# GRU state update: a product and a sum replaced by one running product-sum over interleaved pairs

## The reference, cut to what matters

```python
def cell(h, x):
    gi = x @ W_ih + b_ih
    gh = h @ W_hh + b_hh
    i_r, i_z, i_n = jnp.split(gi, 3, axis=-1)
    h_r, h_z, h_n = jnp.split(gh, 3, axis=-1)
    r = jax.nn.sigmoid(i_r + h_r)
    z = jax.nn.sigmoid(i_z + h_z)
    n = jnp.tanh(i_n + r * h_n)
    h_new = (1.0 - z) * n + z * h
    return (h_new, h_new)
...
x = x + _L3_cond_ref(cond_2048, x, ...)
```

## Time and profile before

| | |
|---|---|
| median of 3 runs | 2069.48 us (2069.31 to 2070.36) |
| the profiled execution, its own time | 2070.81 us |
| its span, first to last instruction | 2069.1 us |
| first and last `h_hi` (L1663) of the 127 in the GRU's steps | 1700.4 us, 2056.0 us |
| mean time of a step between them | 2.82 us |

### The profile page before, as it was taken

The page is one execution under the profiler, slowest core; times in us unless marked ns, Lnnn a source line. Parts: engine busy times, 40 slices in busy tenths (PEclk is TensorE's granted clock), DMA queues, the critical chain, the costliest instruction groups (busy, mean ns, idle before and its releaser), DMA issues. The chain is left out here.

```text
span 2069.1 us, 48431 instructions
## 1 busy us (share of the span) xinstructions
PE 1437.8 (69%) x16570; PEld 1116.0 (54%) x16570; DVE 1418.7 (69%) x6953; ACT 742.6 (36%) x2889; POOL 591.5 (29%) x1597
## 2 busy tenths in 40 slices
PE   6898844444444444445599999999957866677665
PEld 4476533333333333332488888888825754555554
DVE  4457699989989998997556555555546345555554
ACT  4568522222222222223334333433344443333322
POOL 1045355545545554553311111111124000000010
PEclk9979955555555555556799999999988975555555
DMA  3000000000000000002100000000020000000000
GB/s 108 0 1 2 1 2 2 2 3 2 2 3 2 2 2 3 2 2 87 46 1 31 16 18 15 16 1 1 1 81 31 1 0 2 2 2 13 4 11 23
DMA packets 15097, 28.20 MB, mean 14 GB/s; under 512 B 1692, under 2 KB 9464, under 8 KB 14584
## 3 DMA queue, kind: packets, MB, share of 16 engines
q1 hardware_dynamic: 14672, 24.93, 3.5%
q10 hardware_dynamic: 168, 0.04, 0.0%
HBM read 20.77 MB, written 4.19 MB: 12 GB/s over the span
## 5 line engine op out<-in xcount | busy, mean ns | idle before, releaser
L817 PE MATMUL bank<-s_tanh_hi,coup_hi 128*128 128x16 f16 x2048 | 141.6, 180 | 344.6 <-ACT s_tanh_hi L807 329.5
L817 PEld LDWEIGHTS bank<-s_tanh_hi,coup_hi 128*128 128x128 f16 x2048 | 95.0, 108 | 392.0 <-ACT s_tanh_hi L807 376.7
L807 ACT ACTIVATE s_tanh_hi<-s_s 128x32 f16<-128x32 f32 x384 | 88.0, 229 | 394.9 <-DVE s_s L679 394.9
L1245 POOL TENSOR_TENSOR prob<-prob,inv 128x512 f32<-128x512 f32 x64 | 66.5, 1040 | 426.4 <-DVE inv L1211 426.4
L1523 PE MATMUL bank<-h_hi,w_h_hi 128*128 128x16 f16 x1536 | 95.2, 176 | 111.6 <-DVE h_hi L1663 111.6
L1131 ACT ACTIVATE prob<-bank,neg_max 128x128 f32<-128x128 f32 x256 | 90.5, 366 | 215.5 <-DVE neg_max L1180 215.5
L1687 POOL TENSOR_TENSOR x<-x,h 128x32 f32<-128x32 f32 x128 | 34.4, 269 | 447.9 <-DVE h L1666 447.9
L817 PE MATMUL bank<-s_tanh_lo,coup_hi 128*128 128x16 f16 x2048 | 141.3, 180 | 22.3 <-DVE s_tanh_lo L673 9.7
L1523 PEld LDWEIGHTS bank<-h_hi,w_h_hi 128*128 128x128 f16 x1536 | 70.7, 105 | 158.0 <-DVE h_hi L1663 158.0
L817 PE MATMUL bank<-s_tanh_hi,coup_lo 128*128 128x16 f16 x2048 | 130.2, 174 | 0.0
L817 PEld LDWEIGHTS bank<-s_tanh_lo,coup_hi 128*128 128x128 f16 x2048 | 94.6, 107 | 61.9 <-DVE s_tanh_lo L673 33.8
(11 more groups left out here) (286 smaller groups left out, 4713.6 us busy)
## 6 DMA issues: line engine op xcount, KB each, us to landing
w_stage<-in_L_cond_qkv_w_dram SPq DMA_DIRECT2D x12, 512.0 KB, 5.2
x_tok<-in_x_dram SPq DMA_DIRECT2D x4, 512.0 KB, 5.8
ow_stage<-in_L_cond_out_w_dram SPq DMA_DIRECT2D x4, 512.0 KB, 5.4
x_in<-x SPq DMA_DIRECT2D x1, 2048.0 KB, 11.4
x_in_sb<-x_in SPq DMA_DIRECT2D x1, 2048.0 KB, 12.0
out_dram<-o_sb SPq DMA_DIRECT2D x64, 32.0 KB, 1.6
ada_w<-in_L_cond_ada_w_dram SPq DMA_DIRECT2D x1, 1536.0 KB, 12.2
v_bias<-in_L_cond_qkv_b_dram SPq DMA_DIRECT2D x4, 256.0 KB, 5.6
```

What stands on the lines that cost most here:

```text
L807: A.activation(th_hi[:, :], s, ACT.Tanh).then_inc(hi_ready, 1)
L817: ins = nc.tensor.matmul(coupled[:, B * m:B * m + B], w[:, o:o + P], th[:, B * c:B * c + B], start=(first and c == 0 and m == 0), stop=(la ...
L1245: G.tensor_tensor(prob[:, grp % 2, :, :], prob[:, grp % 2, :, :], inv[:, grp % 2, :].unsqueeze(2).broadcast_to([P, HG, T]), MUL).then_inc( ...
```

## The change: what it does

`cand` and `zh` become the even and the odd places of one f32 tile `cand_zh` of 128 x 64, and `keep` the odd places of a tile `zero_keep` whose even places are zero for good. The running product-sum takes state = keep_i * state + cz_i along the 64 places: at an even place the state becomes 0 * state + cand, at the odd place behind it keep * cand + zh, which is h. Its output is a tile of pairs too, whose odd places are h. It is done twice, once with an f16 output (`h_hi`) and once with an f32 output (`h32`). The instruction for `new` and its semaphore go. Readers of `h_hi` (PE, DVE) and of `h32` (DVE, POOL) now read every second element; ACT writes `cand`, and DVE `keep` and `zh`, at every second element. Before the steps there is one memset more.

```diff
-    h32 = [sb(f"h32_{i}", [P, W]) for i in range(2)]
-    h_hi, h_lo = sb("h_hi", [P, W], F16), sb("h_lo", [P, W], F16)
+    cz, kz = sb("cand_zh", [P, W, 2]), sb("zero_keep", [P, W, 2])
+    h32p = [sb(f"h32_{i}", [P, W, 2]) for i in range(2)]
+    h32 = [t[:, :, 1] for t in h32p]
+    h_hip, h_lo = sb("h_hi", [P, W, 2], F16), sb("h_lo", [P, W], F16)
+    h_hi = h_hip[:, :, 1]
+    cand, zh, keep = cz[:, :, 0], cz[:, :, 1], kz[:, :, 1]
+    pairs = lambda t: t[:, :, :].rearrange("p w k -> p (w k)")
...
+            V.memset(kz[:, :, :], 0.0).then_inc(keep_ready, 1)
+            dve.wait_ge(keep_ready, 1)
...
-                V.tensor_scalar(keep[:, :], z[:, :], -1.0, 1.0, MUL, ADD).then_inc(keep_ready, 1)
+                V.tensor_scalar(keep, z[:, :], -1.0, 1.0, MUL, ADD).then_inc(keep_ready, 1)
                 dve.wait_ge(h32_ready, s + 1)
-                V.tensor_tensor(zh[:, :], z[:, :], h32[s % 2][:, :], MUL).then_inc(zh_ready, 1)
-                dve.wait_ge(keep_ready, s + 1)
+                V.tensor_tensor(zh, z[:, :], h32[s % 2], MUL).then_inc(zh_ready, 1)
+                dve.wait_ge(keep_ready, s + 2)
                 dve.wait_ge(cand_ready, s + 1)
-                V.tensor_tensor(new[:, :], cand[:, :], keep[:, :], MUL).then_inc(new_ready, 1)
                 dve.wait_ge(zh_ready, s + 1)
-                dve.wait_ge(new_ready, s + 1)
                 dve.wait_ge(z_full, s + 1)
                 if s + 1 < T:
-                    V.tensor_tensor(h_hi[:, :], new[:, :], zh[:, :], ADD).then_inc(hhi_ready, 1)
+                    V.tensor_tensor_scan(pairs(h_hip), pairs(kz), pairs(cz), 0.0, MUL, ADD).then_inc(hhi_ready, 1)
                 if s >= 1:
                     dve.wait_ge(added, s)
-                V.tensor_tensor(h32[(s + 1) % 2][:, :], new[:, :], zh[:, :], ADD).then_inc(h32_ready, 1)
+                V.tensor_tensor_scan(pairs(h32p[(s + 1) % 2]), pairs(kz), pairs(cz), 0.0, MUL, ADD).then_inc(h32_ready, 1)
...
-                A.activation(cand[:, :], pre[:, :], ACT.Tanh).then_inc(cand_ready, 1)
+                A.activation(cand, pre[:, :], ACT.Tanh).then_inc(cand_ready, 1)
...
-                G.tensor_tensor(x4[:, lap % 2, :, :, j:j + 1], x3[:, :, :, s:s + 1], h32[(s + 1) % 2][:, :].rearrange("p (c b o) -> p c b o", c=C, o=1),
+                G.tensor_tensor(x4[:, lap % 2, :, :, j:j + 1], x3[:, :, :, s:s + 1], h32p[(s + 1) % 2][:, :, 1:2].rearrange("p (c b) o -> p c b o", c=C),
```

More of the change, by code:

```diff
@@ L1433, in gru @@
     gi_n = sb("gi_n", [P, T, C, B])
-    h32 = [sb(f"h32_{i}", [P, W]) for i in range(2)]
-    h_hi, h_lo = sb("h_hi", [P, W], F16), sb("h_lo", [P, W], F16)
+    cz, kz = sb("cand_zh", [P, W, 2]), sb("zero_keep", [P, W, 2])
[5 more added lines that the diff above has]
+    pairs = lambda t: t[:, :, :].rearrange("p w k -> p (w k)")
     r, z = sb("r3", [P, W]), sb("z3", [P, W])
-    rhn, pre, cand, keep, zh, new = (sb(n, [P, W]) for n in ("rhn", "pre", "cand", "keep", "zh", "new"))
+    rhn, pre = sb("rhn", [P, W]), sb("pre", [P, W])
     x4 = sb("x4", [P, 2, C, B, TB])
@@ L1445, in gru @@
     r_ready, z_ready, rhn_ready, pre_ready = sem("r_ready"), sem("z_ready"), sem("rhn_ready"), sem("pre_ready")
-    keep_ready, zh_ready, cand_ready, new_ready = sem("keep_ready"), sem("zh_ready"), sem("cand_ready"), sem("new_ready")
+    keep_ready, zh_ready, cand_ready = sem("keep_ready"), sem("zh_ready"), sem("cand_ready")
     added, o_last = sem("added"), sem("o_last3")
@@ L1628, in gates_low @@
                                        ADD, SUB).then_inc(gil_out, 1)
-            V.tensor_copy(h_hi[:, :], cond).then_inc(hhi_ready, 1)
-            V.tensor_copy(h32[0][:, :], cond).then_inc(h32_ready, 1)
+            V.tensor_copy(h_hi, cond).then_inc(hhi_ready, 1)
+            V.tensor_copy(h32[0], cond).then_inc(h32_ready, 1)
+            V.memset(kz[:, :, :], 0.0).then_inc(keep_ready, 1)
+            dve.wait_ge(keep_ready, 1)
             dve.wait_ge(hhi_ready, 1)
             dve.wait_ge(h32_ready, 1)
-            V.tensor_tensor(h_lo[:, :], h32[0][:, :], h_hi[:, :], SUB).then_inc(hlo_ready, 1)
+            V.tensor_tensor(h_lo[:, :], h32[0], h_hi, SUB).then_inc(hlo_ready, 1)
             for n in range(LAPS):
@@ L1669, in _ @@
                     dve.wait_ge(h32_ready, s + 2)
-                    V.tensor_tensor(h_lo[:, :], h32[(s + 1) % 2][:, :], h_hi[:, :], SUB).then_inc(hlo_ready, 1)
+                    V.tensor_tensor(h_lo[:, :], h32[(s + 1) % 2], h_hi, SUB).then_inc(hlo_ready, 1)
                 if s in unit_at and jobs[s][0] == "gi" and jobs[s][2] < 2 * C:
```

## The result

| | before | after |
|---|---|---|
| median | 2069.31 us (11 runs) | 2075.75 us (11 runs) |
| span of the profiled execution | 2069.1 us | 2073.9 us |
| ratio | | 1.0032, 95% interval 1.0022 to 1.0041 |

What follows compares the result with a forecast made beforehand. The GRU loop's DVE state-update chain, with PE waiting last for `h_lo`, was taken to bound 109 updates; 88 x 0.034 + 21 x 0.089 - 88 x 0.01 = 4.0 us off 2069.5 gave 2065.5 us, range 2054 to 2079.

Steps and rivals of the forecast that it cites:

- A wait comes forward: First running sum must wait for `zh`, which `new` did not: 0.055 us lost on each of 88 updates.
- the first sum holds the engine: Rival: second running sum can't start until the first ends; 5.2 us lost, 2074.7; 0.30 together with a larger fixed part.
- the 88 updates: State updates on the path (109) without the 21 where z was early; forecast to gain 0.034 us each at `h`.
- `new` goes: On DVE, the first running sum could start where `new` stood: 0.28 us gained on each of 109 updates.
- Half pace and overlap: Running sums at 2.02 ns a place, 96 ns more each; the second starts 0.205 us after the first, which still runs.
- The high bound: Running sum at the pace of `gi_lo`, taken as the trace's slowest element, 5 ns: 287 ns more each.
- the far rival: Running sums at 5 ns an element: 42 us slower, 2107; chance 0.05.
- Every second element: Operands stepping by two: only `zh` on the path pays, 0.01 us x 88; POOL's addition nothing.
- Unit steps: 18 GRU steps held by `gi_lo` or ACT's `gi_n`, not by the state update; forecast unchanged.
- POOL's start ahead of `h_lo`'s: POOL's addition starts 0.03 us before `h_lo`, which stays near 280 ns; rival of POOL second: 2055.7, chance 0.08.
- the gain of 0.034: Forecast gain in us at `h`, and with it at `h_lo`, on each of 88 updates, before `zh`'s 0.01.
- the updates with an early z: 21 updates where `new` waited for `cand` and `zh` was done early: no 0.055 us paid, 0.089 us gained each.

Runs made afterwards that it cites:

- waits-alone kernel: Kernel before, with the changed kernel's four waits (keep, cand, zh, z_full) ahead of `new` and only `new`'s wait ahead of `h_hi`: 2076.75 us, ratio 1.0041.
- order-alone: Changed kernel with the same four waits ahead of the first running sum, rewritten so zh's comes first and rides inline: 2065.57 us, ratio 0.9987.
- both pairs: Running sums against plain form, each with fewer waits (0.9960, 0.9972), then also with one semaphore for `h_hi` and `h` (0.9873, 0.9883).
- the best kernel: Changed kernel with two waits ahead of the running sum and one semaphore for `h_hi` and `h`: 2042.38 us, ratio 0.9873.

## Why the prediction was wrong

Its step that failed is "A wait comes forward": "with 0.10 us from end to start it allows 1854.165, 0.055 us after where `new` stood". The place was right and the size was not. I read the 0.10 us off pairs with two or three waits, as if it belonged to DVE, when it belonged to the place of the wait that is released last. Where that wait is inline it is 0.03 to 0.04 us: so `h_hi` behind `new` in the waits-alone kernel, and so, already in the trace of the kernel before, `pre` behind `rhn`:

```profile
1853.32 0.19 DVE L1647 SCALAR_TENSOR_TENSOR rhn<-bank,r 128x32 f32<-128x32 f32 x1 [0.67 <-ACT r L1596]
1853.55 0.19 DVE L1651 TENSOR_TENSOR pre<-rhn,gi_n 128x32 f32<-128x32 f32 x1
```

Where it is a wait instruction with no other behind it, it is 0.09 to 0.10 us; in the changed kernel one more stands behind it, and it is 0.20. So the first running sum began 0.155 us after where `new` stood, not 0.055. The prediction's rival of that sign, "the first sum holds the engine", gives a time close to the measured one, 2074.7, and is refuted: the sums overlap.

Point by point, on the 88 updates:

- *`new` goes*: right, 0.28 us gained.
- *The wait*: 0.155 lost, forecast 0.055. The order-alone and waits-alone kernels show it from both sides.
- *Half pace and overlap*: right. The high bound and the far rival misread the rows: `gi_lo` was not the slowest an element, for in the trace of the kernel before `w_lo` and `ffw_lo` (L1364), with neither an f16 output nor steps, took 2467 and 2637 ns for 512 elements on the mean. At 2.09 ns a place for the running sum nothing hung on it. The starts lie 0.20 to 0.21 us apart in the timeline, 0.205 forecast; the second takes 266 ns where I had 280: 0.014 gained.
- *Every second element*: `zh` cost nothing, where I took 0.01. I had put POOL at nothing, "whose other operands have large steps already"; its addition went from 269 to 288 ns, and `h_lo` ends with it: 0.02 lost.
- *Unit steps* unchanged, but for the update behind them, and *POOL's start ahead of `h_lo`'s*: as forecast.

Sum on a plain step: the gain of 0.034 becomes 0.034 - 0.10 + 0.014 - 0.02 = -0.072 us, and the timeline shows 2.49 for 2.42. On the updates with an early z the wait on `cand` comes last; its instruction holds z_full too and takes 0.05 us where one with a single wait takes 0.02 (the rows of DVEq above), so the running sum starts 0.12 us behind `cand` and not 0.10: about 0.089 - 0.02 + 0.014 - 0.02 = 0.06 gained. 88 x 0.072 - 21 x 0.06 = 5.1 us lost. Only 18 of the 21 waits stand behind unit steps, where z is early; the other three belong to single steps that ran long. Counted so, the sum is 91 x 0.072 - 18 x 0.06 = 5.5 us, and from the first `h_lo` to the last the two traces differ by 5.5 (355.5 and 361.1). The whole spans differ by 4.8, the medians by 6.4 with an interval of 4.6 to 8.5, so what is left over cannot be told from the spread of the runs.

Whether the running sum is worth anything once the waits are right is less sure. It was ahead of the plain form in both pairs, 0.9960 against 0.9972 and 0.9873 against 0.9883, some 2 us each time, and its median step is 0.03 to 0.05 us shorter in the traces (2.33 against 2.37, 2.15 against 2.20); but the intervals of each pair overlap. The 1.3% of the best kernel is otherwise that of the waits and of `h_lo` coming ahead of POOL.

## What to carry to other kernels

In a loop that closes on itself over small instructions, count the wait instructions from the one that is released last up to the instruction it holds: here the first cost 0.06 us and the next 0.10, a third and a half of a 128x32 instruction (0.185). Write the wait that is released last so that it rides on the instruction (in these kernels that was the one written first), let results of one engine that finish in order share a semaphore, and drop a wait that another implies. When two instructions become one, their waits become one list, and a wait that used to be hidden behind the first of them can become the one released last.

## What the runs showed of the hardware

- From the end of one DVE instruction to the start of the one that waits for it: 0.03 to 0.04 us with the wait inline, 0.09 to 0.10 with it on a wait instruction just ahead, 0.20 with another wait instruction (here always one that holds two semaphores) in between. Behind ACT's `cand`, 0.10 with the wait on an instruction just ahead, 0.12 where that one holds two semaphores.
- The running product-sum at 2.09 ns a place beside 1.04 for a plain sum, with overlap between neighbours.
- `h_lo` on DVE and the addition on POOL hold each other up: 281 to 302 ns when POOL's starts first, 191 to 193 when DVE's does. A lead of 0.03 to 0.04 us decides; with `h_lo` first, POOL's rose from 288 to 298 ns, and nobody waits for it.
- An f32 operand at every second element cost DVE nothing that shows (186 for 185 ns), and POOL 20 ns in an addition of 32 elements a partition whose other operands were already spread out.
